# Two thirds of the entropy units move from the projection into the attention blocks of the next image

## The reference: what is computed

```
x = x + attention(gn(x))     # q, k: 24 channels, v: 192; 1x1 convolutions with bias and PReLU
                             # softmax(q^T k) over all 4096 points, times v, in f32
x = x + likelihood(gn(x))    # per channel: a cumulative-logits network of layers 1-3-3-3-1
  lower, upper = logits(x - 0.5), logits(x + 0.5)
  logits: 3 times (softplus(m) @ z + b; z + tanh(f) * tanh(z)), then softplus(m3) @ z + b3
  sign = -sign(lower + upper); max(|sigmoid(sign * upper) - sigmoid(sign * lower)|, 1e-6)
```

## Time and profile before

| | us |
|---|---|
| median of three runs (lowest, highest) | 5517.89 (5516.68, 5522.04) |
| the profiled execution | 5521.67 |
| its span | 5519.9 |
| TensorE busy | 4709.7 (85%) |
| VectorE busy | 4226.4 (77%) |
| ScalarE busy | 2831.0 (51%) |
| GpSimd busy | 1927.4 (35%) |

### The profile page before, as it was taken

One profiled execution on the slowest core, in us unless ns is written; L12 is line 12 of the kernel. 1 busy time (PEld: TensorE's weight loads), 2 busy tenths in 40 slices (PEclk: granted clock), 3 DMA queues, 4 the chain that ended last, 5 costly groups with the idle time before them and its releaser, 6 DMA issues.

```text
span 5519.9 us, 107267 instructions
## 1 busy us (share of the span) xinstructions
PE 4709.7 (85%) x38408; PEld 3126.0 (57%) x38408; DVE 4226.4 (77%) x5378; ACT 2831.0 (51%) x3125; POOL 1927.4 (35%) x1958
## 2 busy tenths in 40 slices
PE   4899779997799878998789987899878998789966
PEld 2678327773277633776237762477525775267721
DVE  4788578875798758886689966788678885789855
ACT  1233773337733377334863348533585335843377
POOL 5433323333333333333333333333323333233312
PEclk8999899998999989999999999999999998999988
DMA  2000340004400143001430014200242002420033
GB/s 60 21 19 13 103 124 14 19 26 105 111 16 15 36 106 101 18 16 39 114 91 14 19 46 122 73 19 13 62 121 59 19 19 70 120 48 16 19 97 93
DMA packets 107368, 305.42 MB, mean 55 GB/s; under 512 B 14401, under 2 KB 14785, under 8 KB 105090
## 3 DMA queue, kind: packets, MB, share of 16 engines
q1 hardware_dynamic: 106818, 298.01, 19.9%
HBM read 230.65 MB, written 50.33 MB: 51 GB/s over the span
## 4 chain that ended last, share of the span: by engine, by line
PE 54%; issue 11%; ACT 11%; DVE 10%; DMA 9%; POOL 3%; SPq 1%; DVEq 0%; ACTq 0%; POOLq 0%
PE ps L1302 10%; PE ps L1304 10%; PE ps L1306 10%; PE ps L1090 6%; PE ps L1253 6%; DMA arena<-x2d 6%; ACT th L659 5%; PE ps L1117 5%; DVE mxp L990 3%; ACT arena L652 3%; DVE arena L985 2%; PE ps L1164 2%; PE ps L1178 2%; PE ps L1147 2%; DMA qst<-shared 2%
## 5 line engine op out<-in xcount | busy, mean ns | idle before, releaser
L1302 PE MATMUL ps<-v_sb,arena 128*128 128x193 f16 x8192 | 2032.9, 248 | 59.0 <-DVE arena L985 59.0
L612 ACT ACTIVATE arena<-ps 128x1024 f32<-128x1024 f32 x1024 | 1046.7, 1024 | 1980.1 <-PE ps L1090 1979.8
L1304 PE MATMUL ps<-v_sb,arena 128*128 128x192 f16 x8192 | 2041.2, 249 | 0.0
L1306 PE MATMUL ps<-v_sb,arena 128*128 128x193 f16 x8192 | 2024.4, 247 | 0.0
L549 POOL CAST arena<-arena 128x1024 f16<-128x1024 f32 x1024 | 1147.6, 1122 | 2006.1 <-ACT arena L612 1983.7
L985 DVE TENSOR_TENSOR arena<-arena 128x1024 f16<-128x1024 f32 x1024 | 1289.4, 1261 | 315.6 <-POOL arena L549 314.5
L990 DVE TENSOR_REDUCE mxp<-ps 128x1 f32<-128x512 f32 x1792 | 1186.5, 688 | 116.5 <-PE ps L1253 105.3
L932 DVE SCALAR_TENSOR_TENSOR th<-th,gates,ps 128x1024 f32<-128x1024 f32 x768 | 953.3, 1277 | 417.0 <-ACT th L659 414.6
L1304 PEld LDWEIGHTS ps<-v_sb,arena 128*128 128x128 f16 x8192 | 801.7, 98 | 265.4 <-issue 6.3
L1302 PEld LDWEIGHTS ps<-v_sb,arena 128*128 128x128 f16 x8192 | 798.7, 97 | 196.1 <-DVE arena L985 47.9
L659 ACT ACTIVATE th<-ps,biases 128x1024 f32<-128x1024 f32 x768 | 821.6, 1119 | 141.2 <-PE ps L1164 109.7
(11 more groups left out here) (122 smaller groups left out, 3470.3 us busy)
## 6 DMA issues: line engine op xcount, KB each, us to landing
arena<-x2d SPq DMA_DIRECT2D x384, 256.0 KB
arena<-x2d SPq DMA_DIRECT2D x384, 128.0 KB, 3.8
xp<-x_dram SPq DMA_DIRECT2D x18, 1536.0 KB, 14.9
shared<-x_dram SPq DMA_DIRECT2D x64, 384.0 KB, 3.6
x2d<-shared SPq DMA_DIRECT2D x64, 384.0 KB, 3.1
res<-x2d SPq DMA_DIRECT2D x96, 256.0 KB
out_dram<-res SPq DMA_DIRECT2D x96, 256.0 KB
kst<-shared SPq DMA_DIRECT2D x32, 256.0 KB, 11.5
```

The costliest lines, as they stand in the source:

```text
L612: act.activation(e_32[:, q % ER, :].rearrange("p (k n) -> p k n", k=2), sc, ACT.Exp).then_inc(full_ready, 1)
L1302: pe.matmul(acc, eh, v_sb[:, m, 0:C + 1], start=(m == 0 and t % 2 == 0), stop=False, skip_group_check=True)
L1304: pe.matmul(acc[:, 0:C], eh, v_sb[:, m, VW:VW + C], start=False, stop=False, skip_group_check=True)
L1306: ins = pe.matmul(acc, el, v_sb[:, m, 0:C + 1], start=False, stop=(m == MT - 1), skip_group_check=True)
```

## The change

Of the 12 units of an image, 0 to 7 (slots 0 to 31) run in the attention blocks of the next image, one unit a block, at spots given by tables (`MAX_AT`, `HIDDEN_AT`, `THIRD_AT`); 8 to 11 (slots 32 to 47) run beside the projection that follows. The last image has a phase A with 16 slots of the image before, and then a new phase C with all its 48 slots. The rest follows from that:

- PSUM: scores have banks 0 and 1 alone. Banks 2 and 3 (T) are shared by maxima and entropy layers; the accumulator pair that is free in a block (F) too.
- The maxima of a block are reduced in pairs, 16 reductions of 128x1024 in place of 32 of 128x512.
- The last layer is computed in four groups of 32 columns in place of two of 64 with two accumulation steps each.
- `t0`, the inputs and the exponentials have memory of their own in place of a shared `arena`; rings are shorter. First tanh works on all partitions at once, and the result and its transfers go in four pieces of 32 partitions.
- In phase A two groups of the first block's maxima stand in each of steps 7 to 14, between the slots.
- The coefficients of the entropy model are computed on GpSimd between the casts of image 0's attention, in place of ahead of it.
- The loop over blocks is written out; the first two images stand ahead of the loop over images.

```
-X4R, T0R, HR1, HR2, XR = 3, 3, 2, 6, 4
-LEAD = 4
+X4R, T0R, HR1, HR2, XR = 2, 2, 2, 4, 3
+LEAD = 3
...
+S_BANK, T_BANK = 0, 2
...
+MAX_AT = {(0, 0): (0, "T"), (0, 1): (1, "F"), (1, 1): (2, "F"), (2, 0): (3, "F"), (3, 0): (4, "T"), (3, 1): (5, "T"),
...
+HIDDEN_AT = {(2, 1): ("h1", 0, "F"), (4, 0): ("h1", 1, "T"), (5, 1): ("h2", 0, "F"), (7, 0): ("h1", 2, "T"),
+             (8, 1): ("h2", 1, "F"), (10, 0): ("h1", 3, "T"), (12, 1): ("h2", 2, "T"), (14, 1): ("h2", 3, "T")}
+THIRD_AT, MAX_TURN_AT, OUT_TURN_AT = (1, 0), (12, 0), (13, 0)
...
+FIRST_MAX_AT = [(2 * (k - 7), 2 * (k - 7) + 1) if 7 <= k < 15 else () for k in range(STEPS + 1)]
...
             def scores(q_col, q):
                 for i in range(2):
                     m = (2 * q + i) % MT
-                    ins = pe.matmul(ps[:, 2 * (q % 2) + i, :], kst[:, m * P:(m + 1) * P],
-                                    qst[:, bass.ds(q_col, N)], start=True, stop=True)
+                    ins = pe.matmul(ps[:, S_BANK + i, :], kst[:, m * P:(m + 1) * P], qst[:, q_col:q_col + N],
+                                    start=True, stop=True)
...
+            def third_layer(l, u, at, reader, n):
...
                 for d in range(2):
-                    for k in range(2):
-                        for h in range(2):
-                            c = 4 * u + 2 * h + d
-                            ins = pe.matmul(ps[64 * h:64 * h + 64, at + d, :], w3[:, u, (1 - k) * UC:(5 - k) * UC],
-                                            th2[:, c % HR2, k, :], start=(k == 0), stop=(k == 1))
+                    for g in range(4):
+                        ins = pe.matmul(ps[32 * g:32 * g + 32, at + d, :], w3[:, u % UNITS, :],
+                                        th2[:, (4 * u + g // 2 * 2 + d) % HR2, g % 2, :], start=True, stop=True)
                 ins.then_inc(h3_mm, 1)
...
+                            spot = (p, i)
...
+                            if more and spot in MAX_AT:
+                                g, name = MAX_AT[spot]
+                                at, reader, n = pair(spot, name)
+                                pe.wait_ge(reader, count(l, reader, n))
...
+                            if third and spot == THIRD_AT:
+                                third_layer(l, j - 1, *pair(spot, "T"))
+                            if hidden and spot in HIDDEN_AT:
+                                kind, n, name = HIDDEN_AT[spot]
+                                if kind == "h1":
+                                    first_layer(l, 4 * j + n, *pair(spot, name))
+                                else:
+                                    second_layer(l, 4 * j + n, *pair(spot, name))
...
+            def phase_c(l):
...
+                for s in range(SLOTS + 2):
+                    if s < SLOTS:
+                        first_layer(l, s, *pair(("h1", s)))
+                    if s % 4 == 1:
+                        third_layer(l, (s - 5) // 4, *pair(("h3", (s - 5) // 4)))
+                    if 1 <= s <= SLOTS:
+                        second_layer(l, s - 1, *pair(("h2", s - 1)))
```

More of the change, by code:

```diff
@@ L27 @@
 BIG = 4096.0
-PER_STEP = 3
 START = 1
@@ L46 @@
 PER_H = UNITS // 2
+IN_B = BLOCKS
 HID = 3
@@ new lines, in last_holder, with block_holder @@
+def last_holder(bank):
+    return next(A_USES[i] for i in range(len(A_USES) - 1, -1, -1) if A_BANKS[i] == bank)
+def block_holder(spot, pair, hidden, third, more, turned):
+    found = None
+    for at in SPOTS[:SPOTS.index(spot)]:
+        if more and at in MAX_AT and MAX_AT[at][1] == pair:
+            found = ("max", MAX_AT[at][0])
+        if hidden and at in HIDDEN_AT and (HIDDEN_AT[at][2] if more else "T") == pair:
+            found = HIDDEN_AT[at][:2]
+        if third and at == THIRD_AT and pair == "T":
+            found = ("h3", -1)
+        if more and at == MAX_TURN_AT and pair == "F":
+            found = ("turn", 0)
+        if turned and at == OUT_TURN_AT and pair == "F":
+            found = ("out", 0)
+    return found
@@ L656, in tanh @@
-                def tanh(kind, c, dst, layer, before, after):
-                    u, d, at = c // 4, c % 2, tile(kind, c)
-                    act.wait_ge(before, l * SLOTS + c + 1)
-                    act.activation(dst, ps[:, at:at + 2, :], ACT.Tanh, bias=biases[:, d, layer, u:u + 1]
-                                   ).then_inc(after, 1)
-                if l is not None:
-                    normalise(l, BLOCKS - 1, 1)
-                if proj:
-                    for n in range(3):
-                        negative(n)
```

1231 lines of the change are left out of this document (678 added, 553 removed).

## The result

The changed kernel takes 6294.11 us (median of four runs, 6292.56 to 6296.94) against 5519.97 for the kernel before in the same session (5516.68 to 5525.52). The ratio is 1.1402, 95% interval 1.1382 to 1.1422: 14% slower. The forecast was 5,637 us, 2% slower, with 5,350 to 5,850 as its range. The direction was right. The size was wrong by 657 us.

What follows compares the result with a forecast made beforehand. Blocks were taken as bound by TensorE with VectorE close behind, the projection stretch by the entropy layers' chain. 5,521.7 + 18 (middle images) - 42 (image 1) - 10 (image 0) + 153 (tail), less 3.8, gave 5,637 us; range 5,350 to 5,850.

Steps and rivals of the forecast that it cites:

- rival A: Attention blocks: hand-overs between TensorE and VectorE cost nothing, a block takes 57.5 us, the whole 5,176; chance 0.24 with part values.
- The walk's waits: Attention blocks: TensorE's waits at second layers, turn of the maxima, first layer and seven other spots, 10.3 us a block.
- so a block takes 66.9: Middle attention blocks: TensorE's work of 56.6 us plus waits of 10.3; bounds 57 and 77.
- Sum 47.5 + 7.3 + 1.8 = 56.6: TensorE's work in a block, us: today's busy time, plus eight hidden slots, plus the last layer of a unit.
- The last block, 53: An image's last attention block, which has no maxima: 53 us.
- Phase A, 155: Middle images, from last denominators to the next image's first value matmul, with 16 slots beside the projection: 155 us.
- block 0, 65: An image's first attention block, priced with no last layer and no output to turn: 65 us.
- 65.5 + 14 = 79.5: Steps 7 to 14 beside the projection: 7 chained steps of 9.35 us, 65.5; the 14 separates full clock, 141, from 155.
- Steps 0 to 7 come to 56: Beside the projection: queries, keys, first values and the wait for the stacks take 56 us.
- The tail, 411: After the last denominators: 16 slots beside nothing, then 48 alone, 411 us, +153; bounds +36 and +236.
- The loop that a lead of 3 makes: Tail: side transfer, first layer, tanhs and issue form a loop of two slots, 12.1 us a half at half clock.
- Rival C: Last layer: groups of 32 columns don't run four at once, 173 us more, some 20 hidden, the whole 5,790; chance 0.12.

Runs made afterwards that it cites:

- experiment 1, e4_reduce_first: Changed kernel with a step's first-half maximum reduction ahead of the previous step's gate on VectorE in the attention blocks: 6093.96 us against 6294.
- experiment 7: Two runs on the changed kernel: turn of the maxima half a step later, 6321.51 us; entropy tanh one step later in an image's last block, 6289.20; against 6294.
- e5_a_side_first: Changed kernel with SyncE issuing side transfers ahead of the residual load that waits for a store, beside the projection: 6289.21 us against 6294.
- e10_a_woven: Changed kernel with values, entropy layers and max groups interleaved in steps 7 to 14 beside the projection, on TensorE and VectorE: 6121.66 us against 6294.
- e8_third64: Changed kernel with the last layer back in two groups of 64 columns, and residual and result in one transfer each: 6263.6 us against 6294.
- b5_pieces: Kernel before with residual and result in four transfers of 32 partitions each, nothing else: 5957.55 us against 5517.96.

## Why the prediction was wrong

The two largest parts of the miss are the middle blocks (point 2, 233 us) and phase A with block 0 (point 4, 227 us).

1. That TensorE and VectorE both come near the length of a block was read rightly, and rival A, hand-overs that cost nothing (57.5), is refuted: a block takes 73.4, and 69.2 with the reductions ahead of the gates. The walk's waits were nearly right too: 10.3 expected, 9.3 found without the transfer and 10.9 with it.
2. The step "so a block takes 66.9" failed by 6.5, and the term that was mis-sized is TensorE's own work: "Sum 47.5 + 7.3 + 1.8 = 56.6", where it is busy for 61.6 in the block shown. Of these 5.0 us 1.6 are the lower clock (experiment 1). About 0.9 are the slots: one takes 3134.90 - 3133.88 = 1.02 between the value matmuls, not the 0.91 that it takes ahead of another slot. Some 1.6 stand at the waits: the last value matmul ahead of each of the 11 has a record of 0.245 us where the next one otherwise starts after 0.083, and the block before had one such place, so 10 x 0.16. This is an estimate, since the ends of matmuls are modelled. About 0.9 is not assigned. The mean of 73.4 holds also blocks like the one of 74.3 at a granted 0.93. In the six middle images this step is 36 x 6.5 = 233 us.
3. The last block, 53, failed by 12.7, six times there: 76 us. I summed TensorE's work and didn't walk the order there. Without maxima a step is short, and TensorE waits for the exponential or for a gate (experiment 7).
4. Phase A, 155, is 179.0 by the prediction's own mark, and block 0, 65, is 78.8: together 37.8 too little, 227 us. The steps with maxima aren't where it failed. Seven of them take 81.3 us in the phase A shown (3627.98 to 3709.31), and 65.5 + 14 = 79.5 was said; there "a third of the stretch at that level" was too little, as a granted 0.74 between the levels of 1.0 and 0.5 means that about half is below, but the sum came out close. What failed is "Steps 0 to 7 come to 56": they take 74.2 in the mean, and in the one shown (3554.34 to 3627.98) the granted clock is 0.81, for which these steps had no term. The last step and the start take 23.4 in place of 20. What makes steps 0 to 7 longer by 18 stays open in part: e5_a_side_first took the wait for a store away and left the time as it was, and e10_a_woven gained 6 us there. Block 0 was priced without a last layer, but one of 1.9 us stands in it (3738.75); beside that its granted clock is 0.89 (2970.64 to 3050.04), and the rows of maxima come up to 3.8 late. That the maxima and values chain with the slots is confirmed by e10_a_woven, which takes it apart.
5. The tail, 411, came out at 452, and two errors stand against each other in that. The loop that a lead of 3 makes was there, but at 12.1 a half it was priced too dear: with single transfers a half takes 10.8 and the tail 377 (e8_third64). The term for SyncE's issue was missing and is worth 75. That the tail with SyncE's order mended, 405, is near 411 is luck.
6. Where an edit was priced at nothing: "the result and its transfers go in four pieces" had no term at all. It is what the lost 440 us of b5_pieces consist of. In the changed kernel it is 75 of the tail and the 42.6 of the late rows; with the longer last layer that comes with single transfers the net is 31. Rival C was aimed at the matmuls of the same edit, which do run four at once: 1.86 us from L1307 to the value matmul behind it (3738.75 to 3740.61). The argument against it, 16 records in 3.65 us, was weak, as that is 0.23 a record and doesn't by itself show two at once.
7. Image 1, 630, came out at 692: 7 in phase A, the rest in its blocks as in points 2 to 4.
8. By the Trainium skill, TensorEngine Tiling (Array Packing), Key Properties, a change of mode drains the TensorE. The trace is in line with that at a small price: 0.11 us a slot, as in point 2. By the Trainium skill, SBUF — State Buffer, Who interferes with whom, a subtraction with two SBUF inputs contends with a GpSimd instruction that reads SBUF. The 1.55 in place of 1.22 us at 3144.61, with a sum and a cast on GpSimd beside it, fits that, but the mean over all rose only from 1.26 to 1.29.

## What to carry to other kernels

Two engines that are each nearly full could share a stretch here (98% and 92% of the block before, with 1.0 us of wait) while its buffers came round slowly; with one pair of banks handed over every half step eleven waits came to 10.9 us a block. So walk the written order spot by spot, in every kind of block, and ask of each wait what the clock does behind it, and what the work costs at the place where it now stands. Count the transfers an edit adds on their issuing queue, by number and not by bytes. If a chain has a transfer's latency on it, a longer lead may be worth more than moving the work: here a gain of 1.1% against a loss of 14%.

## What the runs showed of the hardware

- Issuing a transfer of 32 partitions cost SyncE 0.69 us in one place of the changed kernel (2.76 for four) and 1.6 to 2.0 in b5_pieces, where it issued without a pause, against 0.59 for one of 128 partitions. Four pieces in place of one moved the same 106,818 packets and cost 440 us in the whole.
- Behind a wait of 2.28 us within an otherwise busy block TensorE could run the next matmuls at the lower level (1.04 for two scores in place of 0.59): behind 48 of 64 waits of 2.1 to 2.5 us ahead of a second layer that layer or the scores were longer. Behind 106 waits of under 1.3 us (e4_reduce_first) they never were, and the block's granted clock was 1.00 in place of 0.98.
- Four groups of 32 columns ran at once: 16 records in 1.86 us in place of 3.59 for 16 in groups of 64.
